# A two-layer graph network on one core: a list worked off between two norms, an index copied ahead of a clearing, and attention's blocks normalized inside its loop

## What is computed

```python
h = relu(layernorm(x))
x = x + L0(h)          # relational convolution and a feed-forward
h = relu(layernorm(x))
x = x + L1(h)          # graph attention

# L0: msg = (h @ W_rel)[src, edge_type];  agg = segment_sum(msg, dst)
#     t = gelu(layernorm(agg + h @ W_self + b_conv) * g1 + b1n);  y = h + t
#     return y + gelu(layernorm(y) * g2 + b2n @ W1 + b1) @ W2 + b2
# L1: xt = h @ W.T + bias, 4 heads of 32;  alpha = leaky_relu(a_src[src] + a_dst[dst])
#     ex = exp(alpha - segment_max(alpha, dst));  denom = segment_sum(ex, dst)
#     return segment_sum(xt[src] * ex / (denom[dst] + 1e-16), dst)
```

## Time and profile before

| | |
|---|---|
| median of 3 runs | 4581.68 us (4581.04 to 4583.63) |
| the profiled execution's own time | 4576.85 us |
| its span (first to last instruction) | 4575.1 us |
| busy share of the span: POOL, DVE, PE, ACT | 70%, 55%, 55%, 13% |
| granted TensorE clock, mean | 0.735 of full speed |
| chain that ended last, POOL and issue | 66% and 23% |
| HBM traffic | 68 GB/s over the span |

### The profile page before, as it was taken

How to read it: one execution, slowest core, us unless ns; L and a number is a source line. 1 busy time by engine, 2 the same in 40 slices (tenths; PEclk the granted TensorE clock), 3 DMA queues, 4 the chain that set the end, 5 groups by cost and what they waited for, 6 DMA issues and landing times.

```text
span 4575.1 us, 52415 instructions
## 1 busy us (share of the span) xinstructions
PE 2508.6 (55%) x13797; PEld 2111.2 (46%) x13902; DVE 2517.4 (55%) x6723; ACT 603.1 (13%) x1535; POOL 3194.7 (70%) x3372
## 2 busy tenths in 40 slices
PE   7923444444444444444433666666666666666664
PEld 3423343334434334443423556555555655555553
DVE  5652333333333333333334777777777777777777
ACT  4500111111111111111111000000000000000000
POOL 1077777777777777777746777777777777777772
PEclk9966676667667666766766777777777777877776
DMA  7722222222222222222213222222222222222222
GB/s 255 270 61 53 57 62 57 60 59 57 62 57 62 57 59 59 57 62 57 62 37 102 54 54 54 54 54 54 54 54 54 54 54 54 54 54 54 54 54 76
DMA packets 169389, 311.28 MB, mean 68 GB/s; under 512 B 58788, under 2 KB 99148, under 8 KB 168655
## 3 DMA queue, kind: packets, MB, share of 16 engines
q0 software_dynamic: 107008, 222.77, 20.2%
q1 hardware_dynamic: 46850, 81.19, 4.9%
q10 hardware_dynamic: 15490, 6.87, 0.6%
HBM read 239.51 MB, written 71.09 MB: 68 GB/s over the span
## 4 chain that ended last, share of the span: by engine, by line
POOL 66%; issue 23%; DVE 4%; DMA 3%; PE 2%; ACT 1%; POOLq 0%; DVEq 0%; ACTq 0%; SPq 0%
POOL G L490 66%; DMA rel_table<-G 2%; DMA G<-xt_table,idx 1%; DVE G L857 0%; DVE w L1223 0%; PE bank L1378 0%; PE bank L1379 0%; DVE G L1352 0%; DVE x_res L1354 0%; PE quad L1378 0%; PE quad L1379 0%; DVE edge L1226 0%; PE bank L1420 0%; ACT agg L724 0%; PE quad L1449 0%
## 5 line engine op out<-in xcount | busy, mean ns | idle before, releaser
L490 POOL DMA_INDIRECT G<-rel_table,idx x1680 | 1603.2, 954 | 743.6 <-issue 511.4
L490 POOL DMA_INDIRECT G<-xt_table,idx x1664 | 1570.7, 944 | 543.1 <-issue 502.3
L986 DVE SCALAR_TENSOR_TENSOR agg<-bank,sel,agg 128x128 f32 x208 | 64.2, 349 | 1057.0 <-PE bank L1420 1054.4
L1537 PEld LDWEIGHTS quad<-ident,top 128*128 128x128 f32 x3328 | 576.5, 272 | 143.8 <-issue 141.3
L1537 PE MATMUL quad<-ident,top 128*128 128x128 f32 x3328 | 585.1, 358 | 68.3 <-DVEq L1191 68.2
L1565 PE MATMUL bank<-M,onehot 128*128 128x132 f32 x3328 | 443.9, 289 | 172.5 <-DVE M L1240 172.5
L1565 PEld LDWEIGHTS bank<-M,onehot 128*128 128x128 f32 x3328 | 409.6, 198 | 204.5 <-issue 204.5
L1420 PE MATMUL bank<-G,onehot 128*128 128x128 f32 x1664 | 267.6, 336 | 391.2 <-DMA G<-rel_table,idx 386.8
L1420 PEld LDWEIGHTS bank<-G,onehot 128*128 128x128 f32 x1664 | 263.6, 253 | 395.8 <-issue 395.8
L1553 PE MATMUL bank<-Z,w_all 128*128 128x8 f32 x832 | 173.0, 337 | 442.7 <-issue 436.8
L1553 PEld LDWEIGHTS bank<-Z,w_all 128*128 128x128 f32 x832 | 166.2, 297 | 460.0 <-issue 459.8
(11 more groups left out here) (314 smaller groups left out, 3381.8 us busy)
## 6 DMA issues: line engine op xcount, KB each, us to landing
rel_table<-G SPq DMA_DIRECT2D x98, 512.0 KB, 2.7
G<-rel_table,idx POOLq DMA_INDIRECT x1680, 2.5
G<-xt_table,idx POOLq DMA_INDIRECT x1664, 2.7
xt_table<-w_all SPq DMA_DIRECT2D x25, 264.0 KB, 3.3
x_mid<-X SPq DMA_DIRECT2D x25, 256.0 KB, 2.0
out<-x_res SPq DMA_DIRECT2D x13, 448.0 KB
x_res<-in_x ACTq DMA_DIRECT2D x12, 448.0 KB, 4.4
x_res<-x_mid SPq DMA_DIRECT2D x3, 1792.0 KB, 10.5
```

What stands on the lines that cost most here:

```text
L490: g.indirect_dma_start(out=G[:, s, c, 0:width], out_offset=None, in_=table, in_offset=bass.IndirectOffsetOnAxis(ap=idx[:, s, c:c + 1], axi ...
L986: c.beside(v.scalar_tensor_tensor(row, banks[5 + k][:, 0:D], sel[:, w, bass.ds(g, 1)], row, ALU.mult, ALU.add))
L1537: ins = t.matmul(banks[j][:, hd * P:(hd + 1) * P], top[:, j, hd:hd + 1].to_broadcast([P, P]), ident[:, :], start=False, stop=(hd == HEADS ...
```

## The change

Three things are moved.

- *The list of the first layer.* On DVE it stands inside quad 23 between `quad_second` and `quad_third` (`add_listed`), on PE between `forward` and `project`, on ACT (`repeat_indices`) between `forward` and `third_norm`. The changing of the two tables (`turn_tables`) stands between `quad_third` and `quad_out` of quad 23. DVE's wait for the gather of a list entry is dropped, since PE waits for it.
- *Attention's list index.* DVE gives `rest_free` at once behind `dense_over`, and ACT copies the first list index ahead of the clearing (`listed_index`). The wait for the clearing moves to the first `merge` of the list. DVE no longer waits for the list's gather before it prepares the pass. ACT copies one index more at the end.
- *The normalization.* Once in four rounds of attention, four blocks that no later group touches are divided and added (`finish`) into `A`, 24 times in all, between `nodes` and `scores`. SP stores them from there, 256 KB each; DVE's `finish` waits for the store before it (`s_out`). The wait for the reload comes at the ninth round. Behind the last merge remain the redone quads (into `Y`) and the last four blocks (into `X`). The loop over rounds is cut into two loops with one unrolled body of four rounds between.

```diff
-            for q in range(BATCHES):
-                sp.wait_ge(fin_done, q + 1)
...
+            def store_out(n, lo, tile):
+                sp.wait_ge(fin_done, n + 1)
+                sp.dma_start(out[bass.ds(lo * P, QUAD * P), :].rearrange("(b p) d -> p b d", p=P), tile[:, :, :]).then_inc(s_out, 16)
+            store_out(0, first_of(0), A)
+            with sp.Fori(1, AHEAD) as n:
+                store_out(n, first_of(n), A)
+            n = load_redo_count(sp)
+            with sp.Fori(0, n) as i:
+                store_out(i + AHEAD, load_late(sp, i + 1), Y)
...
                 forward(n)
+                if last and isinstance(n, int):
+                    act.wait_ge(s_plan, 2)
+                    repeat_indices(load_count(act))
...
-            act.wait_ge(dense_over, 1)
-            a.activation(S, ident4[...], ACT.Copy, scale=0.0).then_inc(state_set, 1)
...
+            n = load_count(act)
+            listed_index(0, 1)
+            act.wait_ge(dense_over, 1)
+            a.activation(S, ident4[...], ACT.Copy, scale=0.0).then_inc(state_set, 1)
+            with act.Fori(0, n) as i:
+                ways, passes = load_rest(act, i)
                 with act.Fori(0, ways) as u:
                     att_scalar(listed, passes + u, 1)
+                listed_index(i + 1, i + 2)
...
                 quad_second(n, first_of(n))
-                if not last:
+                if last:
+                    add_listed()
+                else:
                     group_step(g + 3, 1, True)
                 quad_third(n)
+                if last:
+                    turn_tables()
                 quad_out(n, first_of(n))
...
             dve.sem_inc(dense_over, 1)
+            dve.sem_inc(rest_free, 1)
...
-            dve.wait_ge(state_set, 1)
             dve.wait_ge(tables_ready[1], 1)
-            dve.sem_inc(rest_free, 1)
...
-                dve.wait_ge(rest_gathered, i * (16 * CHUNKS) + 16 * CHUNKS)
...
                     edges(listed, c, m, slot, 1, lambda: None)
+                    dve.wait_ge(state_set, 1)
                     merge(listed, c, m, group, first, 1)
...
+            def finish(n, lo, tile, stored):
+                f = S[:, bass.ds(lo, QUAD), :].rearrange("p b (h k) -> p b h k", h=HEADS)
+                c = Chain(dve, c_fin, n * 3)
+                if stored is not None:
+                    dve.wait_ge(s_out, stored)
+                dve_stop(dve)
+                c.step(v.tensor_scalar(inv[:, :, :], f[:, :, :, HC:HD].rearrange("p b h o -> p b (h o)"), 1e-16, None, ALU.add))
+                c.step(v.reciprocal(inv[:, :, :], inv[:, :, :]))
+                c.step(v.tensor_tensor(tile[:, :, :].rearrange("p b (h k) -> p b h k", h=HEADS), f[:, :, :, 0:HC],
+                                       inv[:, :, :].rearrange("p b (h o) -> p b h o", o=1).to_broadcast([P, QUAD, HEADS, HC]), ALU.mult))
+                v.tensor_tensor(tile[:, :, :], tile[:, :, :], x_res[:, bass.ds(lo, QUAD), :], ALU.add).then_inc(fin_done, 1)
...
                 nodes(groups, c, gr, gr, first)
+                if done is not None:
+                    finish(done, first_of(done), A, done * 16 if not isinstance(done, int) or done else None)
                 if landed:
                     scores(groups, c, (s + 1) % SLOTS, 1 - k, landed)
...
+            with dve.Fori(0, LAG) as i:
+                four_rounds(i, None)
+            dve.wait_ge(s_back, 16 * -(-BLOCKS // (2 * WIDE)))
+            four_rounds(LAG, 0)
+            with dve.Fori(LAG + 1, (MAIN - 3) // SLOTS) as i:
+                four_rounds(i, i - LAG)
...
+            n = load_redo_count(dve)
+            with dve.Fori(0, n) as i:
+                finish(i + AHEAD, load_late(dve, i + 1), Y, i * 16 + 16 * AHEAD)
+            finish(n + AHEAD, first_of(AHEAD), X, None)
```

More of the change, by code:

```diff
@@ L683, in self_scalar, with repeat_indices @@
                 a.copy(self_col[:, 0:count * P], banks[0][:, 0:count * P]).then_inc(self_sb, 1)
+            def repeat_indices(repeated):
+                with act.Fori(0, repeated) as i:
+                    group = load_rest_group(act, i + 1)
+                    act.wait_ge(again_gathered, i * (16 * CHUNKS) + 16 * CHUNKS)
+                    act_stop(act)
+                    a.copy(idx[:, MAIN % SLOTS, :], idx_all[:, bass.ds(group, 1), :].rearrange("p a c -> p (a c)")).then_inc(again_idx, 1)
             def quad_scalar(n, lo, last, own):
@@ L1325, in _, with four_rounds @@
             MISSED = STEPS["merge"]
-            with dve.Fori(0, (MAIN - 3) // SLOTS) as i:
+            def four_rounds(i, done):
                 last = load_block(dve, i * SLOTS)
@@ L1505, in quad_tensor @@
                 forward(n)
-                if not isinstance(n, int) or n < AHEAD - 1:
+                if isinstance(n, int) and n == AHEAD - 1:
+                    add_listed()
+                else:
                     add_edges(g + SLOTS - 1, SLOTS - 1, 1, landed(SLOTS - 1))
```

149 lines of the change are left out of this document (68 added, 81 removed).

## The result

The changed kernel takes **4534.84 us** (median of 4 runs, 4530.94 to 4538.96) beside 4581.36 of the kernel before on the same chip (4 runs, 4579.72 to 4583.63): ratio 0.990, 95% interval 0.9887 to 0.9912, 46.5 us less. On another chip it was 4536.05 beside 4580.35 (0.9906, 0.9889 to 0.9922), 44.3 us less. Terms read from the two traces must therefore sum to 37.9, not to 46.5.

What follows compares the result with a forecast made beforehand. POOL's indirect gathers were taken as the bound. Gains of 10.2 (list), 9.4 (index and clearing) and 30.6 (tail), less 7 lost on POOL, sum to 43.2 us: 4581.7 to 4538.5 us, range 4528 to 4553.

Steps and rivals of the forecast that it cites:

- What bounds the kernel: POOL's 1,664 attention gathers, 2076.5 us; an edit counts only if it moves the first, slows POOL or lies behind the last.
- Part 1, the list: Quad 23 to 24 on DVE, PE, ACT: list between two norms ends quad 24 10.2 us earlier, bounds 9 to 11.
- Part 2, index and clearing: Between quad 24 and the first attention gather: 4.6 us instead of 14.0, so 9.4 gained, bounds 7.5 to 10.2.
- Part 3, the tail: Behind the last merge: blocks finished in the loop cut 41.6 us to 9.1; gain 30.6, bounds 28 to 32.
- What the blocks do to POOL: Attention loop: each of 23 finished blocks lengthens one gather by 0.3 us, 7 us lost, bounds 0 and 14.
- undisturbed: Attention loop: finished blocks don't disturb POOL, 4531.5 us; chance 0.22 together with POOL disturbed twice as much.
- 1.9 us once in four rounds fits in DVE's 6.2: Attention loop: a block's 1.9 us on DVE fits in its 6.2 us of gather waits per four rounds, delaying nobody.
- reload and clearing: Attention's start: x_res reload holds POOL 15 us (4553.5), or clearing among others holds first gathers (4548); chance 0.10 together.
- DVE as the bound: Attention round with the finished block: DVE becomes the bound, gains gone from 8.4 us a block, 4596 at 9; chance 0.03.
- The sum: Whole kernel: 10.2 + 9.4 + 30.6 - 7 = 43.2 us faster, 4538.5 us on the median.

Runs made afterwards that it cites:

- list_only: Kernel before with only the list and the table turning moved into quad 23; clearing, index and tail as before: 4567.96 us, ratio 0.9976.
- tail_only: Kernel before with only the blocks finished in the attention loop, front as before: 4556.93 us, ratio 0.9953.
- after_shift: Changed kernel with 88 unexecuted instructions ahead of DVE's second attention loop: ratio 0.9805 on a slower chip; 4536.81 us (0.9905) on one like the first.
- front_only: Kernel before with the list moved between the norms and the index ahead of the clearing, tail as before: 4560.52 us, ratio 0.996.
- the second four runs: Slower chip, 6233.72 us for the kernel before: changed kernel 0.9751, its loop moved 0.9805, the old loop moved 1.0026, changed kernel without four-block stores 0.9760.
- phase_shift: Changed kernel, loop moved by 63 unexecuted increments, with 11 executed semaphore increments ahead of each block's normalization: 4534.25 us, ratio 0.9901.
- after_again_b: The changed kernel itself once more, on a chip like that of the first runs: 4536.05 us, ratio 0.9906.
- pad12: Kernel before with 12 more semaphore increments in the body of DVE's attention loop: 4579.63 us, ratio 1.0001.

## Why the prediction was right

- **What bounds the kernel:** right. Attention is 1,664 gathers back to back after as before, and the first gather, the queue's pitch and the tail make up the difference of the traces to 0.1 us; 2.35 us the other way lie ahead of what was moved.
- **Part 1, the list, 10.2 us:** from the second norm's row to the end of quad 24 it is 2403.29 - 2326.59 = 76.7 us, before 2410.44 - 2324.24 = 86.2: 9.5. The third norm is 8.2 us late, not 7.8, and the open loads 1.95 us, not 1.7. The tables cost nothing. PE's list products took 3.81 us instead of 5.79, but started 2.1 us later behind the second norm than forecast, with their own loads open ahead of them (1.92). `list_only` alone gave 11.3 by its runs, and 10.1 from the second norm to the first gather.
- **Part 2, index and clearing, 9.4 us:** 14.0 - 4.6 = 9.4, to the tenth. The whole front by itself gave 18.8 by its runs, against 19.6.
- **Part 3, the tail, 30.6 us:** 30.2 between last gather and end. Last merge to end is 8.8 us against 9.1; the last round cost 2.6 us against 1.9.
- **What the blocks do to POOL, 7 us lost:** the step with the right size and half of the mechanism. The loss was 8.9, 4.9 and 7.3 us in the three traces that have the blocks and the unmoved loop (`tail_only` is the third), within the bounds of 0 and 14. But not one gather in each of 23 blocks is caught. In the first trace the block's operations lengthen 13, twelve of them to 1.23 or more, which costs 3.7 us and not 7; 25 more are lengthened by the score product, 4.7 us. The prediction named that product only as a reason for its upper bound, and otherwise took it for harmless because of its phase before. That the two together come near 7 is luck. The rival "undisturbed" (4531.5) doesn't hold in these traces: all three have the long gathers.
- **"1.9 us once in four rounds fits in DVE's 6.2":** true for the time, false as told. With the refetch, 2.4 us a turn that no view of before could show, DVE came late enough to wait in a third of its rounds only, and there the score product is no longer held at one phase. The refetch isn't needed for that: in `after_shift_b` the block alone moves DVE, the score product lengthens 24 gathers (2.4 us), the block's operations 23 (3.0 us), and the price is the same within the noise.
- **The rivals** of reload and clearing: `front_only`, which has both, has its gathers at the old 2076.3 us. DVE as the bound needed 8.4 us a block; it took 1.9, and 2.4 for the refetch.
- **The sum:** 43.2 us forecast; 46.5 and 44.3 by the runs, 37.9 between the two profiled executions. By the terms of the traces it is 9.5 + 9.4 + 30.2 - 8.9 = 40.2, less the 2.35 of the later second norm. The runs lie above the forecast and the traces below it, so an agreement closer than some 3 us is not the prediction's merit.

For the step on POOL I matched each attention gather of the changed kernel's trace with the DVE operation under way at its start. Take those with more than 0.15 us of the operation left. In operations with an input in PSUM, up to 2.29 us long (202 starts in the reduction L1234, 169 and 172 in the operations L1264 and L1270 of the changed kernel), they took 0.94 on average, 0.96 at most. In those with two SBUF inputs of 256 or 512 elements (38 starts in L1218, L1351, L1353) they took 0.98 to 1.42; twelve more starts in L1218, with less than 0.1 us left, took 0.94 or 0.95. One of the first kind, with 1.3 us left:

```profile
3379.30 2.29 DVE L1264 TENSOR_TENSOR onehot<-iota,bank 128x2048 f32<-128x2048 f32 x1
...
3380.26 0.94 POOL L502 DMA_INDIRECT G<-xt_table,idx  x1 [0.30 <-issue]
```

**Open:** why the chip of the second four runs gave the change 2.5% and not 1%, and why `after_shift` is slower than the changed kernel there (6116.05 against 6080.38), although it fetches less; neither was tried further. Why TensorE stood idle between matmuls on that chip isn't known. The "7.2 us to landing" of the profile's page is no change in the loop: the profile has landings only for the first gathers of attention, which now run beside the reload (`front_only` has 6.9, `list_only` 2.7), and in the loop the scores start 2.7 us behind their last gather's start as before.

## What to carry to other kernels

When one engine's queue is the bound, list for every operation put beside it whether its inputs lie in SBUF or in PSUM (here gathers took 0.98 to 1.42 us beside two SBUF inputs, and 0.94 on average beside one in PSUM), and at which phase of the queue's pitch it will fall. DVE, which had slack, could be delayed for free here (1 us more a turn, 4534.25 us beside 4536.81), but a delay moves all that follows, and an old operation may begin to collide, as the score product did (one long gather before, 25 after). A tail that is cut up and put under a paced loop keeps most of its gain: 30 us of tail for 5 to 9 us of collisions. After an edit that adds or moves loop code, look at the instruction queue: here one and the same body gave 138 packets at one place and 33 at another, and the body of before 28 and 150.

## What the hardware did that I had not expected

- **A gather that started within one of three VectorE operations on two SBUF inputs (L1218, L1351, L1353) was longer by most of what was left of the operation.** In the changed kernel's trace 0.60 us left cost 0.48 (1.42 instead of 0.94), 0.41 left cost 0.29, 0.22 left cost 0.10: what is left, less 0.1 to 0.2 us, in all 38. In `phase_shift` 0.07 left cost nothing. Beside long operations with an input in PSUM none of 543 took more than 0.96. A gather that had started ahead of the operation wasn't lengthened (in `after_again_b` one from 3453.67 took 0.94, with the score product from 3453.71), nor was one that started 0.03 us into it (the same run, at 2510.75).
- **The same VectorE loop body was fetched anew in each turn at one place and not at another.** The packets of queue 14 had 8192 bytes. With the changed kernel's body of 343 instructions there were 138, at 2.4 us a turn, and 33 with it some 90 instructions further on; in `pad12` a body of that length had 29. Some 60 unexecuted instructions ahead of the body of before took it from 28 packets to 150. My theory that three pages stay and four don't fits every run, but it is an estimate: where the pages begin isn't shown, and the fifth packet of a turn is left open.
- **On one chip TensorE stood idle between matmuls:** up to 2.4 us ahead of single matmuls of 0.38 us, with the granted clock at 0.673 over the run against 0.739 elsewhere, and the same program took 6080 us instead of 4536. The cause is not shown.
